# Splitting a chunk's middle stage around the first half of its large product, and moving one type conversion from VectorE to ScalarE

## The chip, the cores and the metric

The kernel runs on all 8 cores of one Trainium2 chip, two dies of four cores. Each core works on its own two sequences of the batch and exchanges nothing with the others. The metric is the device time in microseconds of the slowest core. The kernel before takes 3226.7 us (median of 3 runs, 3226.34 to 3227.8).

## The reference

The input `x` is 16 sequences of 2048 tokens with 2048 features in fp32. Each token is normalized; one branch is a small recurrent block of rank 8 with a feed-forward part of rank 32, the other a large 2048x2048 product of quantized operands. Their product is added to the input.

```python
xn = layernorm(x)                                   # eps 1e-5
# recurrent branch s
z  = layernorm(xn) * gamma + beta
h  = scan(decay * h + (z @ W_in + b_in))            # rank 8, along the sequence
x2 = xn + (h @ W_out + b_out + z * D_skip)
z2 = layernorm(x2) * gamma + beta
s  = x2 + (relu(z2 @ W_down + b_down) @ W_up + b_up)   # rank 32
# gate g
y  = relu(fake_quant(xn) @ fake_quant(kernel) + fake_quant(bias))
g  = silu(fake_quant(y))                            # 8 bits, one scale for a token
out = x + s * g
```

## The kernel before

A prologue of about 520 us quantizes the kernel matrix into `kq`, which then stays in SBUF. After it the core goes through 32 chunks of 128 tokens (16 for each sequence). A chunk's tokens lie on the 128 partitions.

There is no scheduler. Every operation is recorded by `T` (TensorE), `V` (VectorE), `S` (ScalarE), `G` (GpSimd) or `dma` (queue of SyncE) with the operations that it depends on, and each engine issues its own in exactly the order in which they were recorded; a dependence on another engine becomes a wait on a counting semaphore. So the order of the emit calls in the loop over chunks is the order of each engine. One chunk `c` is made of these pieces:

- `emit_pro(c)`: load of `x`; VectorE's statistics (`L451` to `L477`, a Newton iteration of many 128x1 or 128x2 operations); on ScalarE `xn` (`L486`) and its bf16 copy `xnb` (`L491`); on VectorE the largest magnitude of a token (`L492`) and its scale (`L493` to `L496`); on ScalarE the quantized copy `u8` (`L500`); and the conversion of `u8` to bf16, `qbf` (`L502`), on VectorE.
- `emit_mid(c)`: TensorE transposes `xnb` (`L522`) and `qbf` (`L538`), four 128x128 blocks in one PSUM bank at a time, and ScalarE evicts each bank (`L526` into `xnT`, `L542` into `ixqT`). Then the small products with the columns of `W_in` and `W_down` (`L576`, `L601`, `L611`), the scan (`L634`), and four times a pair of matmuls into `py` (`L661`, `L667`) that VectorE makes into `x2` (`L668`, `L669`). After these comes the second normalization: ScalarE's squares (`L686`), VectorE's sums and Newton iteration (`L689` to `L705`), two transposes of a column of statistics on TensorE (`L706`, `L708`), the 32-row feed-forward vector `hfaug` (`L714` to `L719`), its product with `W_up` in four matmuls (`L732`), and four additions on VectorE that give `s` (`L739`).
- `emit_big_half(c, 0)` and `(c, 1)`: the large product for one half of the output features, 32 matmuls `L764` and two for the bias (`L770`) into the two banks `py`. `emit_big_evacs` is VectorE's evacuation of the two banks with the scale and the maximum (`L783`, `L786`).
- `emit_echunk(c)`: six 128x1 operations on VectorE (`L830` to `L835`), then for each half ScalarE's `qi`, `r`, `g` (`L839`, `L845`, `L848`), GpSimd's product and sum (`L853`, `L857`) and the store.

The loop calls them in this order: middle of `c`, first half and its evacuation, second half, prologue part of `c + 1`, evacuation of the second half, end part of `c`. `py` has two banks for both halves and for the pairs of `x2`, so a half starts only when VectorE has read what was there before.

Of the kernel before, what the change touches and what calls it, by code (L numbers as in the profile page):

```python
# [7 lines left out]
F32 = mybir.dt.float32  # L8
# [3 lines left out]
OP = mybir.AluOpType  # L12
AF = mybir.ActivationFunctionType
# [67 lines left out]
def build_nc(n_seq, seq_len):  # L81
# [33 lines left out]
    def sb(name, shape, dt):  # L115
        return es.enter_context(nc.sbuf_tensor(name, shape, dt))
# [4 lines left out]
    with es:  # L121
# [30 lines left out]
        bdn_t = sb("bdn_t", [32, 1], F32)  # L152
        scal1 = sb("scal1", [8, 4], F32)
        cq128 = sb("cq128", [128, 1], F32)
        bsc = sb("bsc", [1, 8], F32)
        kstat = sb("kstat", [128, 8], F32)
        wint = sb("wint", [128, ND * 8], F32)
# [4 lines left out]
        u8_t = sb("u8", [128, D], U8)  # L162
        qbf_t = sb("qbf", [128, D], BF16)
# [13 lines left out]
        st_t = [sb(f"st{i}", [128, 32], F32) for i in range(2)]  # L177
        nw_t = [sb(f"nw{i}", [128, 8], F32) for i in range(2)]
        nwi_t = [sb(f"nwi{i}", [128, 4], I32) for i in range(2)]
# [50 lines left out]
        def T(deps, fn, inc=False):  # L230
            return P.op("tensor", deps, fn, inc=inc)

        def V(deps, fn, inc=True):
            return P.op("vector", deps, fn, inc=inc)

        def S(deps, fn, inc=True):
            return P.op("scalar", deps, fn, inc=inc)
# [28 lines left out]
        c_haug = V([], lambda e: e.memset(haug[:], 1.0))  # L266
        c_hfau = V([], lambda e: e.memset(hfaug[32:33, :], 1.0))
        c_q128 = V([], lambda e: e.memset(cq128[:], 128.0))
        c_wz = V([], lambda e: e.memset(wcat[:], 0.0))

        p_e = S([L["logit"]], lambda e: e.activation(scal1[:, 0:1], logit[:], AF.Exp, bias=0.0, scale=-1.0))
# [156 lines left out]
        R = [dict() for _ in range(NCH)]  # L428

        def emit_pro(c):  # L430
            rc = R[c]
# [11 lines left out]
            st = st_t[c % 2]  # L443
            tb = t24[c % 2]
            nw = nw_t[c % 2]
            nwi = nwi_t[c % 2]
# [21 lines left out]
            last = n2  # L468
            for _ in range(NEWTON_ITERS):
# [3 lines left out]
                last = V([i3], lambda e: e.tensor_tensor(nwi[:, 2:4].bitcast(F32), nwi[:, 2:4].bitcast(F32), nw[:, 4:6], OP.mult))  # L473
# [25 lines left out]
            dep_u8 = R[c - 1].get("qbf") if c >= 1 else p_bq2  # L499
            rc["q8"] = S([v3, dep_u8, c_q128], lambda e, xn=xn: e.activation(u8_t[:], xn[:], AF.Identity, bias=cq128[:], scale=st[:, 11:12]))  # L500
            dep_qbf = R[c - 1].get("t2b") if c >= 1 else KT0_FREE
            rc["qbf"] = V([rc["q8"], dep_qbf], lambda e: e.tensor_scalar(qbf_t[:], u8_t[:], -128.0, None, OP.add))  # L502
            return

        def emit_mid(c):
            rc = R[c]
            st = st_t[c % 2]
            nw = nw_t[c % 2]
            nwi = nwi_t[c % 2]
# [18 lines left out]
            ixb = ixqT[c % 2]  # L528
            dep_ix_free = R[c - 2].get("bigb") if c >= 2 else (KT1_FREE if c == 0 else None)
            t2e = []  # L530
# [11 lines left out]
                             lambda e, g=g, ixb=ixb: e.activation(ixb[:, 512 * g:512 * (g + 1)], pb2[:], AF.Identity, bias=0.0, scale=1.0)))  # L542
            rc["t2b"] = tlast
            rc["t2e3"] = t2e[3]
            if TRUNC == 22:
                rc["last"] = [t2e[3], t1e[3]]
                return
# [107 lines left out]
            for q in range(NQ):  # L655
                deps_o = [rc["r1a"], p_orhs0, t2e[3]]
                if q == 0:
                    deps_o.append(e1prev[2] if e1prev else (KQ_READY if c == 0 else None))
                else:
                    deps_o.append(prev_a)  # L660
                mo = T(deps_o, lambda e, q=q: e.matmul(py[0][:], r1aug[:], outer_rhs[:, 512 * q:512 * (q + 1)], start=True, stop=True, skip_group_check=True), inc=True)  # L661
                deps_x = [rc["hb"], p_wo, p_wo1]
                if q == 0:
                    deps_x.append(e1prev[3] if e1prev else None)
                else:
                    deps_x.append(prev_b)
                mx = T(deps_x, lambda e, q=q: e.matmul(py[1][:], haug[:], woutaug[:, 512 * q:512 * (q + 1)], start=True, stop=True, skip_group_check=True), inc=True)  # L667
                va = V([mo, rc["xn"], prev_b], lambda e, q=q, xn=xn: e.tensor_tensor(x2tmp[:], xn[:, 512 * q:512 * (q + 1)], py[0][:], OP.mult))  # L668
                vb = V([va, mx], lambda e, q=q: e.scalar_tensor_tensor(  # L669
                    x2_t[:, 512 * q:512 * (q + 1)], x2tmp[:], 1.0, py[1][:], OP.mult, OP.add,  # L670
                    accum_out=st[:, 13 + q:14 + q]))
                prev_a, prev_b = va, vb
                rc[f"x2a{q}"] = va
                rc[f"x2b{q}"] = vb
                rc["xarlast"] = mx
            if TRUNC == 24:
                rc["last"] = [rc["x2b3"], rc["x2a3"]]
                return
            sq = []
            for q in range(4):  # L680
# [3 lines left out]
                else:  # L684
                    deps.append(sq[q - 1])
                sq.append(S(deps, lambda e, q=q: e.activation(sqscr[:], x2_t[:, 512 * q:512 * (q + 1)], AF.Square,  # L686
                                                              bias=0.0, scale=1.0, accum_out=st[:, 17 + q:18 + q])))
# [51 lines left out]
                slast = V([rc[f"wup{q}"], dep_s_free, slast], lambda e, q=q: e.tensor_tensor(  # L739
                    sb_[:, 512 * q:512 * (q + 1)], x2_t[:, 512 * q:512 * (q + 1)], wdst[q][:], OP.add))  # L740
            rc["s1"] = slast
            rc["t2e"] = t2e
            rc["ixb"] = ixb
            return

        def emit_big_half(c, hf_):
            rc = R[c]
            st = st_t[c % 2]
            t2e = rc["t2e"]
            ixb = rc["ixb"]  # L750
            dep_y0 = R[c - 1].get("e1b") if c >= 1 else KQ_READY
            dep_t1free = R[c - 1].get("e2b") if c >= 1 else None
            e1 = rc.setdefault("e1list", [])
            mmlast = None
            for j in range(ND):
                for qq in range(2):
                    fofs = 1024 * hf_ + 512 * qq
                    deps = [t2e[j // 4], KQ_READY]
                    if j == 0 and qq == 0:
                        deps.append(dep_y0 if hf_ == 0 else e1[-1])  # L760
                        deps += [rc["x2a3"], rc["x2b3"]]
                        if c == 0:
                            deps += [p_c8, p_cw2, p_cSe, p_wow]
                    mmlast = T(deps, lambda e, j=j, qq=qq, fofs=fofs, ixb=ixb: e.matmul(  # L764
                        py[qq][:], ixb[:, 128 * j:128 * (j + 1)],
                        kq[:, D * j + fofs:D * j + fofs + 512],
                        start=(j == 0), stop=False, skip_group_check=True), inc=False)
            for qq in range(2):
                fofs = 1024 * hf_ + 512 * qq
                mmlast = T([mmlast, rc["auge"], p_bq2], lambda e, qq=qq, fofs=fofs: e.matmul(  # L770
                    py[qq][:], augrow[c % 2][:], bqrow[:, fofs:fofs + 512],
                    start=False, stop=True, skip_group_check=True), inc=(qq == 1))
            rc[f"big{hf_}"] = mmlast
            if hf_ == 0:
                emit_big_evacs(c, 0)

        def emit_big_evacs(c, hf_):
            rc = R[c]
            st = st_t[c % 2]
            dep_t1free = R[c - 1].get("e2b") if c >= 1 else None  # L780
            e1 = rc["e1list"]
            mmlast = rc[f"big{hf_}"]
            e1.append(V([mmlast, rc["sc0"], dep_t1free], lambda e, hf_=hf_: e.tensor_scalar(  # L783
                t1_t[:, 1024 * hf_:1024 * hf_ + 512], py[0][:], st[:, 12:13], None, OP.mult, OP.max,
                accum_out=st[:, 26 + 2 * hf_:27 + 2 * hf_])))
            e1.append(V([e1[-1]], lambda e, hf_=hf_: e.tensor_scalar(  # L786
                t1_t[:, 1024 * hf_ + 512:1024 * (hf_ + 1)], py[1][:], st[:, 12:13], None, OP.mult, OP.max,
                accum_out=st[:, 27 + 2 * hf_:28 + 2 * hf_])))
            if hf_ == 1:
                rc["bigb"] = rc["big1"]  # L790
                rc["e1b"] = e1[-1]
# [80 lines left out]
        if TRUNC == 0:  # L872
            emit_pro(0)
            for c in range(NCH):
                emit_mid(c)
                emit_big_half(c, 0)
                emit_big_half(c, 1)
                if c + 1 < NCH:
                    emit_pro(c + 1)
                emit_big_evacs(c, 1)  # L880
                if DEBUG_TAPS and c == 0:
                    dsdbg = nc.dram_tensor("dbg_s", [128, D], F32, kind="ExternalOutput").ap()
                    R[0]["tap_s"] = dma("d_t", [R[0]["s1"]], dsdbg[:], s_t[0][:])
                emit_echunk(c)
        elif TRUNC != 1:
            for c in range(NCH):
                if c >= 1:
                    emit_echunk(c - 1)
                emit_pro(c)
                if TRUNC != 21:  # L890
                    emit_mid(c)
                if TRUNC == 3:
                    emit_big_half(c, 0)
                    emit_big_half(c, 1)
                    emit_big_evacs(c, 1)
            emit_echunk(NCH - 1)
        if DEBUG_TAPS:
# [8 lines left out]
            last = R[NCH - 1]["store"]  # L906
            for nm, ap, dt_ in taps:
                dap = nc.dram_tensor(nm, list(ap.shape), dt_, kind="ExternalOutput").ap()
                last = dma("d_t", [last], dap, ap)
# [72 lines left out]
```

How the kernel before makes its waits and increments, by code:

```python
    def emit_engine(self, ename, eng, sems):  # L68
        for o in self.ops:
            if o["eng"] != ename:
                continue
            for k, v in o["waits"].items():
                eng.wait_ge(sems[k], v)
            inst = o["emit"](eng)
            if o["dma"] is not None:
                inst.then_inc(sems[o["dma"]], 16)
            elif o["inc"]:
                inst.then_inc(sems[ename], 1)
# [834 lines left out]
            @block.sync  # L913
            def _(sync):
                P.emit_engine("sync", sync, sems)
                sync.wait_ge(sems["d_o0"], 16 * NCH)
                sync.wait_ge(sems["d_o1"], 16 * NCH)
```

## Time and profile before

| | |
|---|---|
| median of 3 runs | 3226.7 us |
| profiled execution, slowest core | 3247.92 us |
| span of core 3, the slowest, in it | 3246.4 us |
| spans of cores 0 to 3 | 3236.0 to 3246.4 us, mean granted clock 0.665 |
| spans of cores 4 to 7 | 3216.2 to 3219.8 us, mean granted clock 0.684 |
| busy in the span | TensorE 52%, VectorE 35%, ScalarE 22%, GpSimd 9% |
| chain that ended last | TensorE 37%, VectorE 28%, ScalarE 15%, issue 14% |
| DMA | 87.00 MB, mean 27 GB/s |

The profile is of one execution. Busy shares are means over the whole span, and no engine comes near 100%; what matters is the chain of operations through one chunk, in which the engines take turns. In a timeline row the columns are the start in us from the span's start, the time to the end of the row's last instruction, the engine, the line, the operation, output and inputs with their shapes, how many instructions, and in brackets the idle time ahead and what ended it. PEclk is the granted TensorE clock as a share of 2.4 GHz: 0.50 is the level of 1.2 GHz, 1.00 that of 2.4 GHz.

### The profile page before, as it was taken

The numbers are of one execution on the slowest core, as the hardware profiler recorded it, in microseconds if no ns is written. First come the engines' busy times: TensorE is split into PE (matmuls) and PEld (weight loads), VectorE is DVE, ScalarE is ACT, GpSimd is POOL, SyncE is SP. The second block draws the span as 40 slices with busy tenths as digits, with TensorE's granted clock in tenths as the row PEclk, the third lists the DMA queues.
The fourth block names the chain that finished last, engine by engine and source line by source line (L and its number), as shares of the span: only waits on it lengthen the run. The fifth ranks groups of instructions, "written<-read, shape, count | busy, mean of one in ns | idle before, by whom it ended". The sixth has DMA issues, their size and how long they took to land.

```text
span 3246.4 us, 35372 instructions; the slowest of 8 cores (3216.2 to 3246.4 us)
## 1 busy us (share of the span) xinstructions
PE 1672.7 (52%) x6049; PEld 662.7 (20%) x6049; DVE 1121.6 (35%) x3557; ACT 727.8 (22%) x869; POOL 298.6 (9%) x132
## 2 busy tenths in 40 slices
PE   2334335665555555555555555555555555555555
PEld 1222212222121122221122222211212222111121
DVE  4333333333333333333333333333333333333332
ACT  0111122122222222222222212222222222222221
POOL 0000000111111111111110001111111111111111
PEclk9999998555555666655555565555556666666666
DMA  1111210111000000000000000000000000000000
GB/s 37 39 40 45 47 39 1 26 27 27 27 27 27 27 26 27 26 27 26 26 21 13 20 26 27 27 26 27 27 27 27 27 27 27 27 26 26 26 8 20
DMA packets 56530, 87.00 MB, mean 27 GB/s; under 512 B 11118, under 2 KB 44014, under 8 KB 52206
## 3 DMA queue, kind: packets, MB, share of 16 engines
q1 hardware_dynamic: 56348, 84.75, 8.6%
q8 instruction: 93, 1.52, 0.2%
q14 instruction: 89, 0.73, 0.1%
HBM read 51.17 MB, written 33.55 MB: 26 GB/s over the span
## 4 chain that ended last, share of the span: by engine, by line
PE 37%; DVE 28%; ACT 15%; issue 14%; POOL 2%; DVEq 2%; SPq 1%; ACTq 0%; DMA 0%; POOLq 0%
PE py L764 9%; PE pb L538 4%; PE pb L576 4%; PE pb L601 4%; PE pb L611 4%; PE pb L522 3%; DVE x L669 3%; DVE x2tmp L668 3%; ACT xnT L526 2%; DVE t L451 2%; PE pb L411 2%; POOL s L853 2%; PE pb L377 2%; DVE st L492 2%; ACT ixqT L542 2%
## 5 line engine op out<-in xcount | busy, mean ns | idle before, releaser
L764 PE MATMUL py<-kq,ixqT 128*128 128x512 bf16 x2048 | 579.0, 449 | 66.3 <-DVE t L786 66.3
L522 PE MATMUL pb<-eyeb,xnb 128*128 128x128 bf16 x512 | 123.9, 262 | 655.4 <-ACT xnT L526 522.0
L853 POOL TENSOR_TENSOR s<-g,s 128x1024 f32<-128x1024 f32 x64 | 149.8, 2340 | 2926.9 <-ACT g L848 2926.9
L764 PEld LDWEIGHTS py<-kq,ixqT 128*128 128x128 bf16 x2048 | 223.8, 111 | 433.1 <-issue 308.1
L486 ACT ACTIVATE xn<-x,st 128x2048 f32<-128x2048 f32 x32 | 67.1, 2097 | 971.2 <-DVE st L477 971.2
L557 DVE CAST r1aug<-pff 1x128 bf16<-1x128 f32 x32 | 8.9, 279 | 698.0 <-PE pff L556 698.0
L686 ACT ACTIVATE sqscr<-x 128x512 f32<-128x512 f32 x128 | 80.8, 631 | 622.4 <-DVE x L669 622.4
L522 PEld LDWEIGHTS pb<-eyeb,xnb 128*128 128x128 bf16 x512 | 53.0, 104 | 737.2 <-issue 693.9
L538 PE MATMUL pb<-eyeb,qbf 128*128 128x128 bf16 x512 | 125.3, 265 | 109.3 <-ACT ixqT L542 81.0
L857 POOL TENSOR_TENSOR o<-s,x 128x1024 f32<-128x1024 f32 x64 | 149.8, 2341 | 17.5 <-POOL s L853 17.5
L783 DVE TENSOR_SCALAR_CACHE_REDUCE t<-py,st 128x512 f32<-128x512 f32 x64 | 47.9, 748 | 270.4 <-PE py L770 270.4
L601 PE MATMUL pb<-xnT,wcat 128*32 128x128 bf16 x512 | 121.6, 265 | 18.4 <-DVE u_sb L579 17.0
L576 PE MATMUL pb<-xnT,wcat 128*32 128x128 bf16 x512 | 121.9, 265 | 1.6
L611 PE MATMUL pb<-xnT,wcat 128*32 128x128 bf16 x512 | 120.4, 266 | 1.5
L706 PE MATMUL pff<-eyef,st 128*1 128x128 f32 x32 | 11.9, 372 | 197.3 <-DVE st L704 135.0
L542 ACT ACTIVATE ixqT<-pb 128x512 bf16<-128x512 f32 x128 | 76.5, 598 | 158.1 <-PE pb L538 158.1
L839 ACT ACTIVATE qi<-t,st 128x1024 int32<-128x1024 f32 x64 | 73.1, 1143 | 172.4 <-DVE st L835 163.6
L526 ACT ACTIVATE xnT<-pb 128x512 bf16<-128x512 f32 x128 | 75.9, 593 | 128.0 <-PE pb L522 128.0
L414 DVE CAST kq<-pb 128x512 bf16<-128x512 f32 x64 | 44.3, 692 | 161.5 <-PE pb L411 161.5
L492 DVE TENSOR_REDUCE st<-xn 128x1 f32<-128x2048 f32 x32 | 73.2, 2286 | 77.1 <-ACT xn L486 77.1
L661 PE MATMUL py<-outer_rhs,r1aug 2*128 2x512 bf16 x128 | 74.9, 585 | 42.1 <-DVE x2tmp L668 41.5
L669 DVE SCALAR_TENSOR_TENSOR x<-x2tmp,py 128x512 f32<-128x512 f32 x128 | 88.0, 688 | 23.3 <-DVE x2tmp L668 21.4
(193 smaller groups left out, 2094.5 us busy)
## 6 DMA issues: line engine op xcount, KB each, us to landing
x<-L_attn_x SPq DMA_DIRECT2D x32, 1024.0 KB, 6.1
out<-o SPq DMA_DIRECT2D x64, 512.0 KB, 3.4
xn<-L_ffn_kernel SPq DMA_DIRECT2D x128, 64.0 KB, 2.7
s<-L_ffn_kernel SPq DMA_DIRECT2D x128, 64.0 KB, 2.5
wint<-L_attn_W_in SPq DMA_DIRECT2D x16, 4.0 KB
wdnt<-L_attn_W_down SPq DMA_DIRECT2D x16, 16.0 KB
x<-L_attn_W_up SPq DMA_DIRECT2D x1, 256.0 KB
eyef<-c_eye_f SPq DMA_DIRECT2D x1, 64.0 KB
```

Of the source, the lines that this page charges most:

```text
L492: rc["am"] = V([rc["xn"]], lambda e, xn=xn: e.reduce_max(st[:, 10:11], xn[:], axis=AX, apply_absolute_value=True))
L522: tlast = T(deps, lambda e, j=j, b=b: e.matmul(pb2[:, 128 * b:128 * (b + 1)], xnb_t[:, 128 * j:128 * (j + 1)], eyeb[:], start=True, stop=T ...
L526: lambda e, g=g: e.activation(xnT[:, 512 * g:512 * (g + 1)], pb2[:], AF.Identity, bias=0.0, scale=1.0)))
L538: tlast = T(deps, lambda e, j=j, b=b: e.matmul(pb2[:, 128 * b:128 * (b + 1)], qbf_t[:, 128 * j:128 * (j + 1)], eyeb[:], start=True, stop=T ...
L542: lambda e, g=g, ixb=ixb: e.activation(ixb[:, 512 * g:512 * (g + 1)], pb2[:], AF.Identity, bias=0.0, scale=1.0)))
L576: swu = T(deps, lambda e, j=j: e.matmul(pb3[0:32, 0:128], wcat[:, 96 * j:96 * j + 32], xnT[:, 128 * j:128 * (j + 1)], start=(j == 0), stop ...
L601: swA_ = T(deps, lambda e, j=j: e.matmul(pu_A[:], wcat[:, 96 * j + 32:96 * j + 64], xnT[:, 128 * j:128 * (j + 1)], start=(j == 0), stop=Fa ...
L611: swB = T(deps, lambda e, j=j: e.matmul(pu_B[:], wcat[:, 96 * j + 64:96 * j + 96], xnT[:, 128 * j:128 * (j + 1)], start=(j == 0), stop=(j ...
L669: vb = V([va, mx], lambda e, q=q: e.scalar_tensor_tensor(x2_t[:, 512 * q:512 * (q + 1)], x2tmp[:], 1.0, py[1][:], OP.mult, OP.add, accum_o ...
L764: mmlast = T(deps, lambda e, j=j, qq=qq, fofs=fofs, ixb=ixb: e.matmul(py[qq][:], ixb[:, 128 * j:128 * (j + 1)], kq[:, D * j + fofs:D * j + ...
L853: sg = G([e4, rc["s1"], rc.get("tap_s")], lambda e, h=h: e.tensor_tensor(sb_[:, 1024 * h:1024 * (h + 1)], g_t[:], sb_[:, 1024 * h:1024 * ( ...
L857: oo = G([sg, rc["xld"], dep_o_free], lambda e, h=h: e.tensor_tensor(o_t[h][:], sb_[:, 1024 * h:1024 * (h + 1)], xb[:, 1024 * h:1024 * (h ...
```

## The change

`emit_mid` is cut in two behind the pairs of `x2`. The second normalization, the feed-forward part and `s` are now `emit_mid2`. The loop emits the first half of the large product between the two pieces, and the evacuation of that half after `emit_mid2` and not any more inside `emit_big_half`. The conversion `qbf` becomes an activation on ScalarE with a bias column of -128. No operation is dropped and no buffer is added but the column `cm128`.

```diff
@@ emit_pro
-            rc["qbf"] = V([rc["q8"], dep_qbf], lambda e: e.tensor_scalar(qbf_t[:], u8_t[:], -128.0, None, OP.add))
+            rc["qbf"] = S([rc["q8"], dep_qbf, c_m128], lambda e: e.activation(qbf_t[:], u8_t[:], AF.Identity, bias=cm128[:], scale=1.0))
@@ emit_mid
                 rc["xarlast"] = mx
+            return
+
+        def emit_mid2(c):
+            rc = R[c]
+            st = st_t[c % 2]
+            nw = nw_t[c % 2]
+            nwi = nwi_t[c % 2]
             if TRUNC == 24:
@@ emit_big_half
             rc[f"big{hf_}"] = mmlast
-            if hf_ == 0:
-                emit_big_evacs(c, 0)
@@ the loop
             for c in range(NCH):
                 emit_mid(c)
                 emit_big_half(c, 0)
+                emit_mid2(c)
+                emit_big_evacs(c, 0)
                 emit_big_half(c, 1)
                 if c + 1 < NCH:
                     emit_pro(c + 1)
```

TensorE's order in one chunk, from the last pair of `x2` to the second half, in the kernel before (`eyef,st` are the transposes of the statistics, `hfaug` the product with `W_up`, `kq,ixqT` a half of the large product):

```order
L661 MATMUL py<-outer_rhs,r1aug 128x512
L667 MATMUL py<-woutaug,haug 128x512
L706 MATMUL pff<-eyef,st 1x128
L708 MATMUL pff<-eyef,st 1x128
L711 MATMUL pff<-r2row,ones32row 32x128
L713 MATMUL pff<-rm2row,csrow 32x128
L732 MATMUL pb<-wupaug,hfaug 128x512
L732 MATMUL pff<-wupaug,hfaug 128x512 x3
L764 MATMUL py<-kq,ixqT 128x512 x32
L770 MATMUL py<-bqrow,augrow 128x512 x2
L764 MATMUL py<-kq,ixqT 128x512 x32
L770 MATMUL py<-bqrow,augrow 128x512 x2
```

The same place on TensorE in the changed kernel, whose line numbers are a few higher (`L773` is `L764`, `L717` is `L706`, `L743` is `L732`):

```order
L665 MATMUL py<-outer_rhs,r1aug 128x512
L671 MATMUL py<-woutaug,haug 128x512
L773 MATMUL py<-kq,ixqT 128x512 x32
L779 MATMUL py<-bqrow,augrow 128x512 x2
L717 MATMUL pff<-eyef,st 1x128
L719 MATMUL pff<-eyef,st 1x128
L722 MATMUL pff<-r2row,ones32row 32x128
L724 MATMUL pff<-rm2row,csrow 32x128
L743 MATMUL pb<-wupaug,hfaug 128x512
L743 MATMUL pff<-wupaug,hfaug 128x512 x3
L773 MATMUL py<-kq,ixqT 128x512 x32
L779 MATMUL py<-bqrow,augrow 128x512 x2
```

The first half has moved ahead of the six rows of the second normalization and the feed-forward part. VectorE's order did not change there: the evacuation stood behind the four additions of `s` and still does. ScalarE's order at the end of a chunk, where the prologue part of the next chunk (`xn`, `xnb`, `u`) meets the end part of this one (`qi`, `r`, `g`), in the kernel before:

```order
L486 ACTIVATE xn<-x,st 128x2048
L491 ACTIVATE xnb<-xn 128x2048
L500 ACTIVATE u<-xn,cq,st 128x2048
L839 ACTIVATE qi<-t,st 128x1024
L845 ACTIVATE r<-qi 128x1024
```

And in the changed kernel:

```order
L488 ACTIVATE xn<-x,st 128x2048
L493 ACTIVATE xnb<-xn 128x2048
L502 ACTIVATE u<-xn,cq,st 128x2048
L504 ACTIVATE qbf<-u,cm 128x2048
L846 ACTIVATE qi<-t,st 128x1024
```

The conversion now stands between `u` and `qi` on ScalarE. On VectorE, at the same place of the program, the kernel before has this (`t,st<-py,st` is the evacuation of the second half):

```order
L495 TENSOR_SCALAR st<-st 128x1
L496 TENSOR_SCALAR st<-st 128x1
L502 TENSOR_SCALAR qbf<-u 128x2048
L783 TENSOR_SCALAR t,st<-py,st 128x512
L786 TENSOR_SCALAR t,st<-py,st 128x512
```

And the changed one:

```order
L497 TENSOR_SCALAR st<-st 128x1
L498 TENSOR_SCALAR st<-st 128x1
L790 TENSOR_SCALAR t,st<-py,st 128x512
L793 TENSOR_SCALAR t,st<-py,st 128x512
L837 TENSOR_REDUCE st<-st 128x1
```

The evacuation follows the scale directly.

## Rows read from the trace of the kernel before

**Rows 1.** Waits in total, core 3: waiter, releaser, us, times, longest.
```profile
DVE t L783 <- PE py L770: 270.4, 33, 9.6
ACT qi L839 <- DVE st L835: 163.6, 30, 34.3
PE pff L706 <- DVE st L704: 135.0, 22, 6.5
```

**Rows 2.** Timeline of core 3, one chunk, last pair of x2 to next transposes.
```profile
2073.73 0.08 DVE L669 DVE_READ_ACCUMULATOR x<-x2tmp,py 128x1 f32 x1
2074.07 0.58 PE L667 MATMUL py<-woutaug,haug 9*128 9x512 bf16 x1 [0.29 <-DVE x L669]
...
2075.50 0.08 DVE L669 DVE_READ_ACCUMULATOR x<-x2tmp,py 128x1 f32 x1
...
2080.77 0.37 PE L706 MATMUL pff<-eyef,st 128*1 128x128 f32 x1 [6.12 <-DVE st L705]
...
2084.64 0.58 PE L732 MATMUL pb<-wupaug,hfaug 33*128 33x512 bf16 x1 [1.69 <-DVE hfaug L719]
...
2085.40 0.69 DVE L739 TENSOR_TENSOR s<-x,pb 128x512 f32<-128x512 f32 x1 [0.90 <-PE pb L732]
2086.19 2.27 DVE L739 TENSOR_TENSOR s<-x,pff 128x512 f32<-128x512 f32 x3
2086.43 9.98 PE L764 MATMUL py<-kq,ixqT 128*128 128x512 bf16 x32
2096.35 0.69 PE L770 MATMUL py<-bqrow,augrow 1*128 1x512 bf16 x2
2097.31 0.75 DVE L783 TENSOR_SCALAR_CACHE_REDUCE t<-py,st 128x512 f32<-128x512 f32 x1 [8.85 <-PE py L770]
...
2099.11 9.88 PE L764 MATMUL py<-kq,ixqT 128*128 128x512 bf16 x32 [2.06 <-DVE t L786]
...
2112.92 0.15 DVE L496 TENSOR_SCALAR st<-st 128x1 f32<-128x1 f32 x1
2113.06 2.10 ACT L500 ACTIVATE u<-xn,cq,st 128x2048 uint8<-128x2048 f32 x1 [1.22 <-DVE st L495]
2115.33 1.23 DVE L502 TENSOR_SCALAR qbf<-u 128x2048 bf16<-128x2048 uint8 x1 [2.26 <-ACT u L500]
2116.47 0.74 DVE L783 TENSOR_SCALAR_CACHE_REDUCE t<-py,st 128x512 f32<-128x512 f32 x1
...
2119.57 1.15 ACT L839 ACTIVATE qi<-t,st 128x1024 int32<-128x1024 f32 x1 [4.41 <-DVE st L835]
...
2126.91 0.58 ACT L526 ACTIVATE xnT<-pb 128x512 bf16<-128x512 f32 x1
```

**Rows 3.** Windows of core 5: stretch, busy of each engine, PEclk, DMA share, GB/s.
```profile
2072.00:2074.00 2.00, 2.00 (x9) 0.77 (x8) 0.00 (x0) 0.00 (x0) 0.00 (x0) 0.75 0.00 0
2074.00:2076.00 2.00, 2.00 (x11) 0.93 (x10) 0.00 (x0) 0.00 (x0) 0.00 (x0) 1.00 0.00 0
```

**Rows 4.** Timeline of core 5 in the same chunk: the W_up product, both halves.
```profile
2067.97 0.58 PE L732 MATMUL pb<-wupaug,hfaug 33*128 33x512 bf16 x1 [1.70 <-DVE hfaug L719]
2069.76 8.67 PE L764 MATMUL py<-kq,ixqT 128*128 128x512 bf16 x32
2079.23 0.75 DVE L783 TENSOR_SCALAR_CACHE_REDUCE t<-py,st 128x512 f32<-128x512 f32 x1 [7.44 <-PE py L770]
2081.03 7.65 PE L764 MATMUL py<-kq,ixqT 128*128 128x512 bf16 x32 [2.06 <-DVE t L786]
```

**Rows 5.** Timeline of core 3, a weight load at PEclk 0.50.
```profile
2000.88 0.15 PEld L764 LDWEIGHTS py<-kq,ixqT 128*128 128x128 bf16 x1 [0.28 <-issue]
```

**Rows 6.** Window of core 3, second half of the large product, columns as in Rows 3.
```profile
2102.00:2104.00 2.00, 2.00 (x6) 0.70 (x5) 1.46 (x11) 0.00 (x0) 0.00 (x0) 0.53 0.00 0
```

**Rows 7.** Groups by line, ScalarE, prologue and chunks: busy us, mean ns.
```profile
L397 ACT ACTIVATE xn<-u,kstat 128x2048 f32<-128x2048 uint8 x8 | 16.8, 2097 | 1.6 <-ACT u L394 1.6
L491 ACT ACTIVATE xnb<-xn 128x2048 bf16<-128x2048 f32 x25 | 47.8, 1911 | 3.9 <-ACT xn L486 0.4
```

More of the change, by code:

```diff
@@ L154, in build_nc @@
         cq128 = sb("cq128", [128, 1], F32)
+        cm128 = sb("cm128", [128, 1], F32)
         bsc = sb("bsc", [1, 8], F32)
@@ L268, in build_nc @@
         c_q128 = V([], lambda e: e.memset(cq128[:], 128.0))
+        c_m128 = V([], lambda e: e.memset(cm128[:], -128.0))
         c_wz = V([], lambda e: e.memset(wcat[:], 0.0))
@@ L544, in emit_mid @@
             rc["t2e3"] = t2e[3]
+            rc["t2e"] = t2e
+            rc["ixb"] = ixb
             if TRUNC == 22:
@@ L741, in emit_mid @@
             rc["s1"] = slast
-            rc["t2e"] = t2e
-            rc["ixb"] = ixb
             return
@@ L891, in build_nc @@
                     emit_mid(c)
+                    if "last" not in R[c]:
+                        emit_mid2(c)
                 if TRUNC == 3:
                     emit_big_half(c, 0)
+                    emit_big_evacs(c, 0)
                     emit_big_half(c, 1)
```

## The prediction

> **What bounds the kernel now.** I read the busy shares first: no engine is above 52% of the span, so the time is that of a chain in which the engines take turns. The waits in total [rows 1] name three turns that the change touches, each once in a chunk: VectorE waits for a half of the large product (270.4 us), ScalarE waits for the last of the 128x1 operations before `qi` (163.6 us), and TensorE waits for the second normalization (135.0 us in the 22 cases put down to `L704`; the others are put down to the next line). The timeline of one chunk of core 3 shows how they follow each other [rows 2]. The last quarter of `x2` is done at 2075.58 (2075.50 + 0.08). TensorE then has nothing until 2080.77, waits again for `hfaug`, does the four `W_up` matmuls from 2084.64, the first half from 2086.43, and VectorE evacuates it from 2097.31. The statistics of the next chunk follow on VectorE, then ScalarE's `xn` and `u8` (2113.06), VectorE's `qbf` (2115.33) and the second evacuation (2116.47), and `qi` starts at 2119.57. ScalarE's eviction of the next transposes is queued behind the end part, at 2126.91. DMA is nowhere in this chain.
>
> **The first half ahead of the second normalization.** From the end of `x2` to the first evacuation a chunk now takes 2097.31 - 2075.58 = 21.73 us [rows 2]. It is 5.19 (squares, sums, Newton, all with TensorE idle) + 3.87 (first transpose 2080.77 to first `W_up` matmul 2084.64) + 1.79 (`W_up` to `L764`) + 10.88 (`L764` to evacuation, 0.27 of it VectorE's start behind the last bias matmul at 2097.04).
>
> In the changed order TensorE starts the half as soon as the last `x2` quarter is there. The nearest gap from VectorE to TensorE is 0.26 us (2073.81 to 2074.07, the pair before) [rows 2]. Then come the 10.61 us of the half with its bias, the 3.87 us, 0.76 us from the first `W_up` matmul to the first addition of `s` (2084.64 to 2085.40), and the four additions, 3.06 us (2085.40 to 2088.46). The two evacuations are queued behind these additions on VectorE, and their matmuls are long done. Sum 0.26 + 10.61 + 3.87 + 0.76 + 3.06 = 18.56 us: 3.17 us less in each of 32 chunks, 101 us. So of the 5.19 us of stall that are now covered, 2 come back: the additions of `s` used to lie beside the large product and now stand in front of its evacuation. The 5.19 us of statistics have twice their length of cover. Without it (a half under 5 us) they would be late again; no row is near that.
>
> **The clock in the first half.** On core 5 the granted clock was 0.50 until about 2073 and 1.00 after (mean 0.75 in the window from 2072) [rows 3]. That is 3.2 us after `L764` started there (2069.76), but 5.0 us after the first `W_up` matmul (2067.97), and TensorE had no gap between the two [rows 4]. In the changed order the half has in front of it only the pairs of `x2` with gaps. If the busy stretch that raises the clock began with `W_up`, the rise comes 1.79 us later in the half. At 0.50 one matmul takes 0.43 us (0.15 + 0.28) [rows 5], at 1.00 0.24 us (7.65 / 32) [rows 4], so a us more at the low level costs 1 - 0.24/0.43 = 0.44 us: 0.8 us per chunk. From the other side, a half that core 3 started with little work ahead and at a low clock (2099.11) was still at 0.53 in the window to 2104, over 4 us after its start [rows 2, 6]. Ends: 0 (rise as now) and 5.4 us (never: 34 x 0.43 + 0.27 = 14.9 against 9.47 from 2069.76 to 2079.23). I take 0.8 us, the value nearest to the one rise that I can place against both starts: 26 us in all. Working the other way, the small matmuls and `W_up` may now run at the high level, since they follow the half; a 512-column matmul would give back 0.19 us, the transposes little. I take 0, with 0.3 us per chunk as the end.
>
> **The second half** will start about 8 us after the first ends, with the `W_up` stretch the only denser work between, so it too begins at the low level, and takes what a first half takes now, or what core 3's did here (9.88) [rows 2]. It lies beside the statistics of the next chunk: VectorE isn't ready for its evacuation before 2113.07 (`L496`), and the half with its bias ended at about 2109.6. 3.5 us of cover, so nothing, except in the last chunk, where it is on the path: 1 us once. The Trainium skill ("TensorE: Matmul & The Clock Gate", section on HAM oscillation) warns that matmul bursts cut apart by waits each pay the slow start anew. The change makes one burst into two, and by that rule alone, if both were on the path, the 1 us would be paid 31 more times, and the sum would end near 3113; the row shows the second one covered.
>
> **The conversion on ScalarE.** Now `qi` starts 6.51 us behind `u8` (2113.06 to 2119.57): ScalarE is busy for 2.10 and idle for 4.41, waiting for VectorE's `qbf`, two evacuations and six small operations [rows 2]. From the evacuation's start to `qi` are 3.10 us (2116.47 to 2119.57). With `qbf` gone, VectorE can evacuate at 2113.1, so its part is ready at 2116.2. ScalarE itself has `u8` (2.10), a start-up of 0.15 as between any two dependent ones, and the conversion. No 128x2048 conversion from uint8 to bf16 is in the chunks; the nearest are 1911 ns (fp32 to bf16, no columns as operands) and 2097 ns (uint8 to fp32, two columns) [rows 7]. I take 2.00, between. `qi` then starts 2.10 + 0.15 + 2.00 - 0.10 = 4.15 us behind `u8` (independent activations overlap by about 0.1). That is 2.36 us less, in 31 chunks, 73 us; now ScalarE itself is what is late, by 1.1 us over VectorE. Ends 2.26 and 2.45. In the first chunk nothing of an end part is behind it, and the eviction of the first transposes waits for the conversion: 2 us once.
>
> The Trainium skill ("ScalarE: Activation LUTs", Rules for kernel authors) gives plain additions to VectorE, not ScalarE. For the instruction alone the trace agrees: 1.23 us there against some 2.00 here. By that rule the move costs 0.8 us in each of 31 chunks, 24 us, in place of the gain of 73. It would hold if the conversion's time on ScalarE came on top; the 4.41 us of idle time say that it goes into a gap.
>
> **The sum.** 101 - 26 + 73 - 1 - 2 = 145 us. Against the profiled execution (3247.9, of which 3246.4 is the span) that gives 3103. The median of the runs is 21 us below that execution; the slower die there had a mean clock of 0.665 against 0.684 and was 24 us behind the other. The terms don't depend on that, so I take them from the median: 3226.7 - 145 = 3082 us.
>
> **Rivals.**
> *The clock rises as early in the half as now, and the small matmuls behind it gain too* (20%). For it: the pairs of `x2` are 512 columns wide as well. Against: there was no rise at the pairs up to now. 32 x (3.17 + 0.3) + 73 - 3 = 181: 3046 us.
> *It rises much later, some 3.8 us over now* (15%), as the start without work ahead on core 3 hints [rows 6]. 1.7 us lost in a chunk: 32 x 1.47 + 73 - 3 = 117: 3110 us.
> *The conversion's move brings nothing* (4%): the second evacuation would turn out to wait for the second half itself, grown longer at a low clock, or the activation be far over 2.1 us. It needs the half to end 2.3 us later than VectorE is free, so some 6 us later than now. 75 - 3 = 72: 3155 us; with the 24 us of the rule above 3179.
> *Both halves stay at the low level throughout* (2%). TensorE then works in shorter bursts with a long gap between, and no half reaches the high level. The first half costs 5.4 us more against 3.17 gained, the last chunk's second half 6.4 more: 32 x (3.17 - 5.4) + 73 - 2 - 6.4 = -7: 3233 us, slower. It decides from about 5.4 us of added time in a first half. Against it: every half that I looked at reached the higher level within 5 us.
> That the order isn't what the change says is excluded by the order of the instructions.
>
> **How the numbers follow.** The forecast has 59%, with a range of its own from 3062 to 3100: the bounds of the conversion are 3 us each way, the rest is where in the half the clock rises. With the two clock rivals 94% is covered; the range takes in both and some margin for die 0 at a reduced clock, 3040 to 3122. About 0.2% is what a measurement of this kernel can tell from no change. All but the last rival are far beyond that: faster 0.97, same 0.01, slower 0.02.
>
> **What would show it.** In the changed profile TensorE's `L773` starts 0.3 us behind the last quarter of `x2`; the first transpose `L717` follows the bias matmuls without a gap; the four additions end right where the evacuation `L790` starts, so its wait for the product is gone (now 270 us, then only that of the second halves, near 0). From the end of `x2` to `L790` I expect 18.6 to 19.5 us. The second half shows PEclk 0.50 at its start. ScalarE's `L504` takes 1.9 to 2.1 us, the wait of `L846` for VectorE (163.6 us) nearly vanishes, and `L846` starts 4.2 us behind `L502`. The prediction is wrong in its first part if the first half takes over 13 us, and in its second if `L846` still waits for VectorE.

## The result, and the profile after

The changed kernel takes 3060.6 us (median of 9 runs), the kernel before 3226.9 us (median of 10). The ratio is 0.949, with a 95% interval of 0.946 to 0.952. That is 166 us less; forecast were 145. The time lies just below the forecast's own range (3062 to 3100) and nearer to the first clock rival (3046) than to 3082. In the profiled execution the cores' spans are 3056.7 to 3059.1 us.

To see where the time went, I cut a chunk into five stretches and took the mean over the 31 that have a next chunk, from instruction starts in the timeline of core 5, which before ran at the undisturbed clock levels ("end of `x2`" is the end of its last quarter):

| stretch | before | forecast | after |
|---|---|---|---|
| end of `x2` to first evacuation | 20.35 | -2.37 | 17.02 (-3.33) |
| to `u8` (`L500`, now `L502`) | 15.88 | 0 | 15.91 |
| to `qi` (`L839`, now `L846`) | 6.55 | -2.36 | 4.20 (-2.35) |
| to `r1aug` (`L557`, now `L561`) | 22.04 | 0 | 22.43 (+0.39) |
| to the next end of `x2` | 20.67 | 0 | 20.66 |
| chunk | 85.48 | -4.73 | 80.23 (-5.25) |

31 times 5.25 are 163 us; the prologue is 2.5 us longer. From the last end of `x2` to the end of the kernel it is 49.7 us and not 50.6: the first stretch gains 2.45 us there too, but the second half, which nothing covers in the last chunk, takes 8.60 us in place of 7.69. That makes the 161 us between core 5's two spans (3219.0 and 3057.8). The medians, of the slowest core, are 166 us apart.

The waits in total on core 5 after the change. Those of VectorE for the product and of `qi` for VectorE [rows 1] are left only once each; new on the list is `r2row`, the reader of the first transpose, which now waits for the first half:

```profile
DVE r2row L718 <- PE pff L717: 155.4, 32, 5.8
PE py L773 <- DVE x L673: 35.1, 32, 1.4
ACT qi L846 <- DVE st L842: 31.2, 1, 31.2
DVE t L790 <- PE py L779: 9.5, 1, 9.5
```

The timeline of core 5, one chunk, at the place of [rows 2], from the last quarter of `x2` to the second half:

```profile
2045.19 0.08 DVE L673 DVE_READ_ACCUMULATOR x<-x2tmp,py 128x1 f32 x1
...
2045.42 9.87 PE L773 MATMUL py<-kq,ixqT 128*128 128x512 bf16 x32 [1.08 <-DVE x L673]
...
2055.75 0.27 PE L717 MATMUL pff<-eyef,st 128*1 128x128 f32 x1
...
2059.47 0.58 PE L743 MATMUL pb<-wupaug,hfaug 33*128 33x512 bf16 x1 [1.80 <-DVE hfaug L730]
...
2060.22 0.69 DVE L750 TENSOR_TENSOR s<-x,pb 128x512 f32<-128x512 f32 x1 [0.90 <-PE pb L743]
2061.01 2.27 DVE L750 TENSOR_TENSOR s<-x,pff 128x512 f32<-128x512 f32 x3
2063.20 0.74 DVE L790 TENSOR_SCALAR_CACHE_REDUCE t<-py,st 128x512 f32<-128x512 f32 x1
...
2064.99 8.63 PE L773 MATMUL py<-kq,ixqT 128*128 128x512 bf16 x32 [3.66 <-DVE t L793]
```

The half starts 0.15 us behind `x2`, the first transpose follows it without a gap, and the evacuation starts where the additions end: 17.93 us in all here, and my sum was 17.95 for core 5 (0.26 + 9.20 + 0.80 + 3.87 + 0.76 + 3.06). But this is a chunk with a long first half (9.87 us). In the chunks that I looked at, long halves alternate with halves of about 8.5 us.

The conversion, same core, at the place where `qi` used to wait 4.41 us [rows 2]:

```profile
1998.11 2.09 ACT L502 ACTIVATE u<-xn,cq,st 128x2048 uint8<-128x2048 f32 x1 [1.27 <-DVE st L498]
1998.18 0.75 DVE L790 TENSOR_SCALAR_CACHE_REDUCE t<-py,st 128x512 f32<-128x512 f32 x1
...
2000.41 2.00 ACT L504 ACTIVATE qbf<-u,cm 128x2048 bf16<-128x2048 uint8 x1 [0.20 <-DVE st L838]
...
2001.09 0.15 DVE L842 TENSOR_SCALAR st<-st 128x1 f32<-128x1 f32 x1
2002.32 1.13 ACT L846 ACTIVATE qi<-t,st 128x1024 int32<-128x1024 f32 x1
```

VectorE is ready for `qi` at 2001.24, ScalarE at 2002.3: the conversion goes into the old wait with 1.1 us to spare on VectorE's side, as worked out.

### The profile page after: what moved, and what is told of

Its sections match the earlier page's. It is cut to its first block, busy times and chain, and to the rows that moved or that the text cites. A ratio compares the mean times of both kernels' runs of the same rounds, so it can differ in the third digit from the quotient of the medians.

```text
span 3059.1 us, 35308 instructions; the slowest of 8 cores (3056.7 to 3059.1 us)
## 1 busy us (share of the span) xinstructions
PE 1655.6 (54%) x6049; PEld 665.0 (22%) x6049; DVE 1081.8 (35%) x3526; ACT 788.6 (26%) x901; POOL 298.6 (10%) x132
## 4 chain that ended last, share of the span: by engine, by line
PE 37%; DVE 28%; issue 15%; ACT 15%; POOL 3%; DVEq 2%; SPq 1%; ACTq 0%; DMA 0%; POOLq 0%
PE py L773 10%; PE pb L540 4%; PE pb L580 4%; PE pb L615 4%; PE pb L605 4%; PE pb L524 3%; DVE x L673 3%; DVE x2tmp L672 3%; POOL s L860 3%; ACT xnT L528 3%; DVE t L453 2%; PE pb L413 2%; PE pb L379 2%; ACT ixqT L544 2%; ACT xn L488 2%
## 5 line engine op out<-in xcount | busy, mean ns | idle before, releaser
L773 PE MATMUL py<-kq,ixqT 128*128 128x512 bf16 x2048 | 583.1, 455 | 156.7 <-DVE t L793 121.6
L773 PEld LDWEIGHTS py<-kq,ixqT 128*128 128x128 bf16 x2048 | 228.4, 112 | 523.9 <-issue 359.9
L561 DVE CAST r1aug<-pff 1x128 bf16<-1x128 f32 x32 | 8.9, 279 | 748.1 <-PE pff L560 748.1
L673 DVE SCALAR_TENSOR_TENSOR x<-x2tmp,py 128x512 f32<-128x512 f32 x128 | 88.0, 687 | 23.3 <-DVE x2tmp L672 20.7
L672 DVE TENSOR_TENSOR x2tmp<-xn,py 128x512 f32<-128x512 f32 x128 | 88.1, 688 | 21.3 <-DVE x L673 20.5
L540 PEld LDWEIGHTS pb<-eyeb,qbf 128*128 128x128 bf16 x512 | 53.2, 104 | 194.2 <-issue 150.7
L671 PE MATMUL py<-woutaug,haug 9*128 9x512 bf16 x128 | 75.8, 593 | 30.8 <-DVE x L673 30.8
```

Of the source, the lines that this page charges most:

```text
L540: tlast = T(deps, lambda e, j=j, b=b: e.matmul(pb2[:, 128 * b:128 * (b + 1)], qbf_t[:, 128 * j:128 * (j + 1)], eyeb[:], start=True, stop=T ...
L673: vb = V([va, mx], lambda e, q=q: e.scalar_tensor_tensor(x2_t[:, 512 * q:512 * (q + 1)], x2tmp[:], 1.0, py[1][:], OP.mult, OP.add, accum_o ...
```

## The experiments

Theory S says that the parts are constants that add up. Theory P says that the chunk doesn't choose the moment at which TensorE's clock rises, so that each us saved elsewhere shifts the rise within the first half and is partly paid back there, or doubled. All times are medians of 4 runs, with the kernel before run beside them on the same chip (medians 3225.9 us for the first four experiments, 3221.7 and 3223.7 us for the others). Ratios are against these. Differences to the changed kernel's 3060.6 us are not from one chip, and a few us of them can be that.

**Only the split.** The changed kernel with

```diff
-rc["qbf"] = S([rc["q8"], dep_qbf, c_m128], lambda e: e.activation(...))
+rc["qbf"] = V([rc["q8"], dep_qbf], lambda e: e.tensor_scalar(qbf_t[:], u8_t[:], -128.0, None, OP.add))
```

> Only the split: the first half of the large product ahead of the second normalization, the conversion qbf stays on VectorE. Theory S (the parts of the change simply add): the stretch from the end of x2 to the first evacuation becomes 3.3 us shorter in each chunk as in the changed kernel (20.4 to 17.0 on core 5), the stretch from u8 to qi stays 6.5, and the time is 3226.9 - 107 = 3120 us. Theory P (the moment at which TensorE's clock rises is not set by the chunk, so a shorter chunk shifts it within the first half, and what a part gains depends on where it lands): chunk times even at 81.9 us, one of the two gaps between rises that the changed kernel shows, so 3226.9 - 31 x 3.5 = 3118 us. The total can't tell them; the evenness of the chunks can: under S the first half takes 8.4 and 9.8 us in turn as in the changed kernel, under P it takes one value throughout. Both expect the transposes L538 to keep their 0.84 us gaps, if the 0.1 us more that they have in the changed kernel belongs to the conversion's move.

3112.4 us, ratio 0.967 (0.964 to 0.970), 113.5 us less than before. Windows of core 5, columns as in [rows 3], each around a rise inside a first half:

```profile
1589.00:1590.00 1.00, 1.00 (x5) 0.37 (x4) 0.63 (x4) 0.00 (x0) 0.00 (x0) 0.72 0.00 0
1671.00:1672.00 1.00, 1.00 (x5) 0.39 (x4) 0.60 (x4) 0.00 (x0) 0.00 (x0) 0.76 0.00 0
1753.00:1754.00 1.00, 1.00 (x5) 0.41 (x4) 0.63 (x4) 0.00 (x0) 0.00 (x0) 0.80 0.00 0
```

In a window of 1 us a mean PEclk of 0.72 places the change from 0.50 to 1.00 at 0.56 us: the rises are at 1589.56, 1671.48 and 1753.40, 81.92 us apart each time. The chunks are 82.0 us, and from the eighth on the first stretch stays at 16.5 to 17.3. In the changed kernel it swings between 16.2 and 18.2. So it is as even as theory P has it, though both theories' totals (3120 and 3118) were 6 to 8 us too high. The stretch from `qi` to `r1aug` is 22.07, so the 0.39 us belong to the conversion.

**Only the conversion.** The kernel before with the `S` line in place of the `V` line.

> Only the conversion qbf on ScalarE, the order of before. From u8 to qi 4.2 us in place of 6.55 and 0.4 us more in the transposes (their gaps 0.94 and not 0.84). Theory S: (2.35 - 0.39) x 31 - 2 = 59 us less, 3168 us, and the first half takes 8.4 to 8.7 us on an undisturbed core, as before. Theory P: the first half, which this kernel does not touch, gets longer, since the chunk of 83.5 us fits no spacing of the rises that the traces show (78.5, 81.9, 85.3): its time becomes uneven between 8.4 and 9.9, mean about 0.5 us over before, and the kernel takes about 3182 us.

3191.4 us, ratio 0.989 (0.988 to 0.991): 34.5 us less, where adding constants gives 59. Windows of core 5 around rises:

```profile
1549.50:1550.50 1.00, 1.00 (x5) 0.44 (x4) 0.00 (x0) 0.00 (x0) 0.00 (x0) 0.86 0.00 0
1634.50:1635.50 1.00, 1.00 (x5) 0.43 (x4) 0.00 (x0) 0.00 (x0) 0.00 (x0) 0.70 0.00 0
1716.50:1717.50 1.00, 1.00 (x4) 0.35 (x3) 0.13 (x1) 0.00 (x0) 0.00 (x0) 0.73 0.00 0
```

Rises at 1549.78, 1635.10 and 1717.04: the gaps are 85.3 and 81.9, no longer even. The stretch from `u8` to `qi` is 4.21 as expected. The stretch from `x2` to the first evacuation, which this kernel leaves untouched, went from 20.35 to 20.95, with values from 20.0 to 21.7; its half takes 9.15 us in place of 8.61, where theory S left it alone. So a saving of 2.35 us arrives as 1.2: 0.6 goes to the clock and 0.4 to the transposes. Split and conversion alone give 148 us, together 166. They don't add, as theory P has it; the 45 us that P gave for the conversion were still 10 too many.

**A delay.** The changed kernel with one more operation in the chain behind `x2b_`:

```diff
+if c >= 1:
+    x2b_ = V([x2b_], lambda e: e.tensor_tensor(x2tmp[:], x2_t[:, 0:512], x2_t[:, 512:1024], OP.add))
```

> The changed kernel with one more VectorE operation (128x512 sum into the idle scratch x2tmp, some 0.7 us, 0.85 us with its start) in each chunk's chain of statistics. Theory S: 31 x 0.85 = 26 us more, 3087 us. Theory P: chunks of 79.1 and 81.4 us in turn become even ones of 81.9, the spacing of rises that is now just in reach: 31 x 1.7 = 52 us more, 3113 us, and the first half takes 9.3 to 9.9 us in every chunk.

3104.9 us, 44 more than the changed kernel: between the two theories' 26 and 52. The stretch with the operation grew by 0.82 us, the first stretch by 0.6 (17.02 to 17.64), and most chunks last 81.4 to 82.4 us, with short spells at 80.1 to 81.2. A us added costs 1.7 here.

**The evacuation first.**

```diff
 emit_mid2(c)            # without the additions of s
 emit_big_evacs(c, 0)
+emit_s(c, range(4))     # the four additions, moved here
 emit_big_half(c, 1)
```

> The changed kernel with the two evacuations of the first half ahead of the four additions of s on VectorE, everything else as it is. The second half can start 3.1 us earlier. If the second half is covered by the statistics of the next chunk, as the prediction says, nothing comes of it: VectorE does the same work ahead of those statistics, 3060 us, within 10. If TensorE with its two halves is what the chunk waits for, most of the 3.1 us comes back: 2965 to 2985 us.

3032.0 us, ratio 0.940 (0.939 to 0.942): 28.6 us less than the changed kernel, outside what both theories gave. VectorE of core 5:

```profile
2043.28 0.21 DVE L730 TENSOR_SCALAR hfaug<-hfv 32x128 bf16<-32x128 f32 x1 [0.18 <-DVE hfv L728]
2043.55 0.75 DVE L794 TENSOR_SCALAR_CACHE_REDUCE t<-py,st 128x512 f32<-128x512 f32 x1
```

The evacuation starts 0.06 us behind `hfaug`. In the changed kernel VectorE idles there for 0.90 us, until the first `W_up` matmul has landed. From the end of `x2` to `u8` it is 32.1 us against 32.9. In 31 chunks that is 25 us, the filled wait. The 3.1 us by which the second half starts earlier bring nothing in these chunks, which is what the cover said. Only the last chunk, whose second half is on the path, is 4.2 us shorter from the end of `x2` (45.5 for 49.7).

**The order of two waits.** In the `qbf` transposes:

```diff
-deps = [rc["qbf"], L["eyeb"]]
+deps = [L["eyeb"], rc["qbf"]]
```

> The changed kernel with the two waits of the qbf transposes (L540) in the other order: first the wait for the constants, long satisfied, then the one for ScalarE. In the kernel before the wait for ScalarE came last, since qbf was awaited from VectorE ahead of it; with the conversion on ScalarE the two waits for ScalarE are one, and the wait for the constants stands behind it. Theory W (a satisfied wait behind the one that is released last costs 0.1 us each time): the gaps in front of these groups go from 0.94 back to 0.84, the stretch from qi to r1aug from 22.4 to 22.05 us, 12 us less by the sum, 3048, of which the clock may take or add some. Rival (the transposes are slower because ScalarE now writes what they read, or because of what the DMA does there): nothing changes, 3060 us.

The transposes on core 4, first of the changed kernel:

```profile
2017.66 1.02 PE L540 MATMUL pb<-eyeb,qbf 128*128 128x128 bf16 x4 [0.94 <-ACT ixqT L544]
```

and then with the waits exchanged:

```profile
2010.96 1.03 PE L540 MATMUL pb<-eyeb,qbf 128*128 128x128 bf16 x4 [0.84 <-ACT ixqT L544]
```

The gap is 0.84 again, and the stretch to `r1aug` 22.02 us. Theory W holds. The median (3059.7) doesn't show it, since the slowest core counts: in the profiled run cores 2 and 3 had a mean granted clock of 0.665 and spans of 3067. Cores 4 to 7 have 3045.3 to 3051.6, against 3056.7 to 3057.9 in the changed kernel. The one of the four runs in which all eight cores had 0.675 to 0.677 took 3048.3 us, as expected.

**No satisfied waits.** In `finalize` each engine remembers what it has waited for:

```diff
+seen = {}
+for o in self.ops:
+    for k, v in list(o["waits"].items()):
+        if seen.get((o["eng"], k), 0) >= v:
+            del o["waits"][k]
+        else:
+            seen[(o["eng"], k)] = v
```

> The changed kernel without the waits that an earlier wait of the same engine on the same semaphore has already satisfied. Theory I (these waits cost TensorE issue time at every matmul): the small products L580, L605, L615, 48 matmuls at 0.24 us, get shorter by up to half, the stretch from r1aug to the end of x2 goes from 20.7 to between 15 and 18.5 us, the gaps ahead of the transposes to 0.84 or less, in all 2880 to 2980 us. Rival (weight load and matmul themselves take the 0.24 us): only the 0.1 us of each of the eight groups of transposes, 31 x 0.8 = 25 us less, 3036 us.

2701.2 us, ratio 0.839 (0.837 to 0.841), below the range of theory I. The first of the small products, first in the changed kernel (core 5), then here (core 4):

```profile
2025.44 3.81 PE L580 MATMUL pb<-xnT,wcat 128*32 128x128 bf16 x16
```

```profile
2001.22 1.89 PE L587 MATMUL pb<-xnT,wcat 128*32 128x128 bf16 x16
```

A window of that core there, columns as in [rows 3]:

```profile
2001.00:2003.00 2.00, 1.97 (x17) 1.71 (x17) 0.00 (x0) 0.00 (x0) 0.00 (x0) 0.50 0.93 303
```

Sixteen matmuls take half the time, at the low clock level in both. The stretch from `r1aug` to `x2` is 13.9 and not 20.7 us, the one from `qi` to `r1aug` 18.7 and not 22.4. The page of the profile counts 22716 instructions in place of 35308. TensorE was held by its own instruction stream, which I hadn't seen: busy rows without idle time looked like work. The 2701.2 us hold a lower clock on some cores as well: in the profiled run cores 2 and 3, which had only the two levels 0.50 and 1.00, have spans of 2674.6 and 2677.7, the slowest cores (mean clock 0.702 to 0.707) 2690.8 to 2693.0.

**Work ahead of the half.** Behind each pair of `x2`:

```diff
+for _d in range(2):
+    T([], lambda e, q=q, ixb=ixb: e.matmul(pb2[:, 0:256], ixb[:, 128 * q:128 * (q + 1)], kq[:, 512 * q:512 * q + 256], ...))
```

> The changed kernel with two idle matmuls 128x256 (from ixqT and kq into the free bank pb2) behind each of the four pairs of x2, whose results nobody reads. Theory D (dense work ahead of the first half raises the clock earlier): the clock rises before or at the start of the first half, its time goes from 8.4 to 9.8 in turn to below 8.4 throughout, the stretch to the first evacuation from 17.0 to 15.5 to 16.3 us; the pairs themselves lose up to 0.5 us. 3010 to 3045 us. Rival (only the half itself raises it): the first half stays at 8.4 to 9.8 us, and the added matmuls cost 0 to 0.5 us a chunk, 3060 to 3076 us.

3082.7 us, ratio 0.957 (0.954 to 0.959). On core 2, nearly undisturbed, the first stretch is 16.94 against 17.03 and the pairs cost 0.24 us more. A first half of core 3 and the window of its rise:

```profile
2052.22 8.41 PE L776 MATMUL py<-kq,ixqT 128*128 128x512 bf16 x32 [0.63 <-DVE x L673]
```

```profile
2054.50:2055.50 1.00, 1.00 (x5) 0.34 (x3) 0.59 (x4) 0.00 (x0) 0.00 (x0) 0.76 0.00 0
```

The rise is at 2054.98, 2.8 us behind the start. Over all chunks of this core the rises come 2.5 to 5.9 us behind it (2.7 to 5.8 in the changed kernel), and the half takes 9.09 us in the mean (9.10). So the rise did not come clearly earlier. These added matmuls don't help; the rest of the added time is a lower granted clock (0.81) on some cores.

**The additions later.** Three additions of `s` behind `x2b_` in the next prologue part, in the wait for `xn`, and the fourth behind the scale.

> The changed kernel with the four additions of s taken out from ahead of the first evacuation: three of them stand in VectorE's wait for xn in the next chunk's prologue part, the fourth behind the scale of u8. The term of the prediction that it tests is that of the 5.2 us of covered stall 3.1 come back as these additions. If so, x2 to q8 gets 3.1 + 0.8 us shorter (the 0.8 as in the run where the evacuation stood first: VectorE's wait for the W_up product is filled as well), 29.0 us in place of 32.9, and the kernel takes 3060 - 31 x 3.9 = 2940 us, within 25 for the clock. If the second half were late then, since the stretch that covers it is as long as before but starts earlier, u8 and qi would be held by its evacuation, and most of it would be lost: 3000 to 3040 us.

2965.7 us, ratio 0.920 (0.917 to 0.922). From `x2` to `u8` 29.3 us on core 4 (13.35 + 15.98) against 29.0 expected. 95 us less, of 121; in the profiled run one die had a clock of 0.671 to 0.681 and spans of 2949.6 to 2963.8, the other spans of 2941.7 to 2944.3. Against the changed kernel's 3056.7 to 3057.9 on the same four cores that is 114 us.

**Together, and on the kernel before.** The two edits combined, the leaving out of waits on the kernel before, and one step further: the transposes of chunk `c + 1` emitted ahead of the end part of chunk `c`.

```diff
 emit_big_evacs(c, 1)
+if c + 1 < NCH:
+    emit_mid_t(c + 1)   # the transposes, their evictions and augrow
 emit_echunk(c)
```

> The kernel before, without the change, but without the waits that an earlier wait of the same engine has already satisfied. It asks whether the change is still worth its 5% once TensorE's issue is free of them. Theory A (the change and the waits are apart, since the waits are in the prologue, the transposes and the small products and the change is in the second normalization and at u8): 2701 + 166, or 155 with the 0.4 us of the wait order gone, so 2856 to 2867 us. Theory B (where the clock rises decides what the change is worth): the same within 40 us either way, with the first halves uneven. If the large product itself were held by these waits, the first half would be shorter than 8.4 us on an undisturbed core.

2861.0 us, ratio 0.887 (0.885 to 0.889). Against the 2701.2 us of `elide` the change is worth 160 us without the waits, which is what theory A gave. But that is partly the lower clock of `elide`: its two undisturbed cores (2674.6 and 2677.7) are some 182 us below these (2856.7 to 2859.2), and a chunk goes from 75.1 to 69.2 us. The first halves here are uneven (8.9 to 9.8 us on core 5), as theory B expected.

> The changed kernel with both edits: the satisfied waits left out, and the four additions of s in VectorE's waits of the next prologue part. If they add, 2701 - 31 x 3.1 = 2606 us, within 20. If the second half of the large product is now late (TensorE's chain got shorter elsewhere, but the cover behind the second half has not changed), 2640 or more.

2545.4 us, ratio 0.789 (0.787 to 0.791), 156 us below `elide` and not 95. A chunk went from 69.19 us (core 3) and 69.76 (core 5) to 65.03 (core 5); of the 4.16 us against core 3, 3.88 lie between the end of `x2` and `u8`. The clock blurs both medians: on undisturbed cores alone `s_late` gains 114 us on the changed kernel, and this kernel (2541.8 to 2543.9) 133 us on `elide` (2674.6 and 2677.7). So of the 61 us beyond the 95 some 40 are slower cores in the medians of the two earlier runs, and some 19 are left.

> As the run before, and the transposes of the next chunk with their evictions are put ahead of the end part (qi, r, g, the product and sum on GpSimd, the store), which ScalarE then does while TensorE has the small products. Theory C (the end part's 7.3 us on ScalarE stand in the chain only because the evictions of the transposes are queued behind them): from u8 to r1aug 15.5 us in place of 22.8, 2606 - 31 x 7.3 = 2380 us. Rival: the end part comes between the transposes and the squares of x2 and delays these, or the load of x, which waits for the end part, comes late for the statistics: 2450 to 2600 us.

2395.9 us, ratio 0.743 (0.741 to 0.745), the fastest of all. From `u8` to `r1aug` 15.4 us in place of 22.8. But the stretch with the small products now takes 16.0 us and not 13.5, so the step brings 150 us and not the 226 of theory C. That the time still came within 16 us of the 2380 is luck: the run that it builds on was 61 us faster than the 2606 in that sum. A piece of core 5's timeline:

```profile
1548.73 2.34 POOL L889 TENSOR_TENSOR s<-g,s 128x1024 f32<-128x1024 f32 x1 [49.55 <-ACT g L884]
1548.99 2.17 DVE L658 TENSOR_SCALAR u_sb<-u_sb,c 8x128 f32<-8x128 f32 x1
...
1551.34 2.53 POOL L893 TENSOR_TENSOR o<-s,x 128x1024 f32<-128x1024 f32 x1 [0.27 <-POOL s L889]
1551.83 2.12 DVE L674 CAST haug<-h 8x128 bf16<-8x128 f32 x1
```

VectorE's 8x128 operation takes 2.17 us beside GpSimd's product, and the cast 2.12 beside GpSimd's sum; in the run before the same two took 0.27 and 0.22. Each ends 0.1 us behind GpSimd's operation.

## Why the prediction was right, and where it was off

The two mechanisms, a covered half and a filled wait, came as forecast. The total is nearer than its parts: the first stretches gained some 30 us more than forecast, the transposes lost 12 us that the prediction hadn't counted, and only the difference shows.

- **The order and the stall.** As said: the statistics are covered, 2 of the 5 us come back as additions ahead of the evacuation. The expected 18.6 to 19.5 us from `x2` to `L790` were missed (17.0 in the mean, 16.2 to 18.2 on core 5): they were built on core 3's half of 9.98 us, where core 5's took 8.67, and on the clock term below. `evac_first` and `s_late` show these terms singly.
- **The second half is covered.** Shown by `evac_first`: 3.1 us earlier, no gain from it. It started at the low level in every chunk of core 5, and takes 8.4 to 9.8 us, 9.12 in the mean against 7.83 before. Only the last chunk pays for that, 0.9 us for the 1 us forecast.
- **The conversion.** 2.35 us against 2.36, 2003 ns on core 3 (2001 on core 5) against 2.00 us. `L504` starts 0.21 us behind the end of `u8`, for which 0.15 was taken; that `qi` was at 6.55 us and not 6.51 on core 5 evens it out. The rule that the prediction names from the Trainium skill ("ScalarE: Activation LUTs", Rules for kernel authors), plain additions to VectorE, is right for the instruction (1.23 us against 2.00) and would have misled for the kernel.
- **The clock term was mis-sized, and its reason was wrong.** I took 0.8 us per chunk, on the ground that the `W_up` matmuls had opened the busy stretch. Two first halves of the changed kernel on core 5 speak against it, and the windows of their rises:

```profile
1724.63 9.83 PE L773 MATMUL py<-kq,ixqT 128*128 128x512 bf16 x32 [1.08 <-DVE x L673]
1805.89 8.47 PE L773 MATMUL py<-kq,ixqT 128*128 128x512 bf16 x32 [1.08 <-DVE x L673]
```

```profile
1730.00:1731.00 1.00, 1.00 (x5) 0.44 (x4) 0.00 (x0) 0.00 (x0) 0.00 (x0) 0.87 0.00 0
1808.50:1809.50 1.00, 1.00 (x6) 0.39 (x5) 0.58 (x5) 0.00 (x0) 0.00 (x0) 0.86 0.00 0
```

  The rise came 5.6 us after the start in one (1730.26) and 2.9 us in the other (1808.78), with the same work ahead of both. 2.9 is as early as before, without `W_up` in front. In the kernel before the rises were evenly apart:

```profile
1560.50:1561.50 1.00, 1.00 (x5) 0.41 (x4) 0.00 (x0) 0.00 (x0) 0.00 (x0) 0.74 0.00 0
1646.00:1647.00 1.00, 1.00 (x5) 0.44 (x4) 0.00 (x0) 0.00 (x0) 0.00 (x0) 0.83 0.00 0
```

  (1561.02 and 1646.34, 85.32 apart.) In the changed kernel they alternate between 81.9 (1730.26 from 1648.34) and 78.5. The Trainium skill ("TensorE: Matmul & The Clock Gate", Part 1: The HAM clock gate) says that the observation which sets the clock runs freely and does not start with the work; these rises agree. Its cost was 0.4 us per chunk in the half and not 0.8 (core 5, from the start of `L773` to that of `L717`: 9.59 us in the mean of all chunks, 8.85 to 10.34, against 9.20 in the chunk read before).
- **Small terms taken at nothing.** From the first transpose to `W_up` it is 3.69 and not 3.87 us in the mean, and from `W_up` to the first addition 0.64 and not 0.76, since these small matmuls follow the half at the high level (`L717` 0.27, before 0.37). The start behind `x2` is 0.15 and not 0.26, and the evacuation starts 0.08 before the additions' end. With the 0.4 us by which the clock cost less than forecast these make up 0.9 of the 0.96 us by which the first stretch gained more. The first clock rival had the 0.3 us of the small matmuls right, and the early rise in every other chunk.
- **A cost that I missed.** 0.39 us in the transposes, 12 us in all. The conversion's new engine changed which semaphores the transposes wait for, and so the order of the waits; `wait_order` shows it.

## What to carry to other kernels

In a chain in which engines take turns, move the long independent piece over the short dependent ones, and then look at what stands ahead of its evacuation on the in-order engine. Count the waits that each instruction carries: those already satisfied can cost as much as the work (1.9 of 3.8 us for sixteen small matmuls), and the one likely to be released last should stand last. And where the clock rises inside the work, a chunk's parts need not add: measure the whole.

## What the runs showed that I had not expected

- Leaving out satisfied waits gives 359 us on the changed kernel (some 381 on undisturbed cores) and 363 on the one before, more than twice the change itself.
- A satisfied wait behind the released one costs 0.10 us (0.94 against 0.84) for each of four groups of transposes in a chunk.
- VectorE operations of 0.27 us (8x128) and 0.22 us (the cast behind it) last over 2 us when GpSimd works beside them: 2.17 and 2.12 in `late_end`. The Trainium skill ("Trainium Architecture — The Big Picture", What this means for kernel authors) says that the two engines share a port pair and that its use is an exclusive lock; these rows agree.
